# An AdaLN feed-forward kernel on one Trainium2 core: other engines and banks for the last two of 32 tiles

## The chip, the core and the metric

The kernel runs on one core of a Trainium2 chip. Its engines run instruction streams of their own and meet only at semaphores: TensorE (PE, matmuls, with PEld for its weight loads), VectorE (DVE), ScalarE (ACT), GpSimd (POOL) and SyncE (SP), which here does nothing but issue DMAs, in order, on its queue (SPq). SBUF is the on-chip memory of 128 partitions; PSUM holds matmul results in eight banks of 128x512 f32. The metric is the device time of one execution in microseconds (us).

## What is computed

Tokens are a matrix of 4096 rows (2 batches of 2048) by 512. A conditioned matrix product gives h; a feed-forward block with ternary weights and activations rounded to 8-bit steps per row follows, and x is added back.

```python
def _act_quant(x):
    scale = 127.0 / jnp.clip(jnp.max(jnp.abs(x), axis=-1, keepdims=True), 1e-05)
    xq = jnp.clip(jnp.round(x * scale), -128.0, 127.0) / scale
    ...
def _bitlinear(x, w):
    return jnp.einsum('bsi,oi->bso', _act_quant(x), _weight_quant(w))
gate = jax.nn.silu(_bitlinear(x, w_gate))
up = _bitlinear(x, w_up)
return _bitlinear(gate * up, w_down)
...
x = x + _L0_ffn_ref(_L0_cond_ref(x, cond_8, L0_cond_weight, ...), ...)
```

w_gate and w_up are 2048 by 512, w_down is 512 by 2048. The step that matters here is the second `_act_quant`: the row maximum over all 2048 columns of gate * up must be known before any of it can be rounded and multiplied by w_down.

## The kernel before

The 4096 rows are 32 tiles of 128 rows. A first phase (to about 125 us) builds the conditioned weights, makes the weights ternary and produces the rounded, transposed activations qT of nearly all tiles. The second phase goes through the tiles, one step each, and every engine has its own hand-written order with semaphore counts; there is no scheduler. The tile index is s, its parity par picks one of two buffers.

In a step each of the four chunks (512 of the 2048 inner columns) goes this way. TensorE (`chunk`, L498) multiplies qT by the gate and the up weights into PSUM banks GATE + c % 2 and UP + c % 2. ScalarE (`silu_chunk`, L269) applies silu to the gate bank. VectorE (`step`, L400) multiplies it with the up bank into `prod` and takes the chunk's absolute maximum (L402). TensorE starts a chunk only when silu and product of two chunks before it are done.

After four chunks VectorE combines the maxima and computes the row's scale in four small operations (L412, L414, L417, L419), rounds `prod` in place in two halves of 1024 columns by adding a large constant (L424), and computes `out_unit` (L426). ScalarE (`convert`, L276) subtracts the constant and writes bf16 into the single buffer `q2`, half by half; in the next step this stands between silu chunks 0 and 1. SyncE (L211) issues one DMA transpose for each half into `q2T`. TensorE (`down`, L508) then does sixteen matmuls into bank DOWN + par, interleaved with the chunks two tiles later. VectorE (`finish_out`, L390) scales that bank and adds x (`x_res`) into `result`; this runs in the middle of the step three tiles later.

SyncE's order around a step s (`step` of the sync block, L205 to L220) is: both transposes of tile s - 1; wait for the result of tile s - 3; its store (L218); the load of x for tile s - 1 into the same buffer (L220). All of it is one queue: an instruction that waits holds all behind it.

For the last tiles nothing differs in the kernel before, but that TensorE runs out of chunks: behind chunk (31, 3) come the down matmuls of tiles 29, 30 and 31 in a row. Names in profile rows: `wc` is the big buffer in which prod, q2, q2T and silu lie, `ps` is PSUM.

Of the kernel before, what the change touches and what calls it, by code (L numbers as in the profile page):

```python
# [7 lines left out]
ALU = mybir.AluOpType  # L8
# [5 lines left out]
TILES = BATCH * SEQ // P  # L14
# [10 lines left out]
COND_BANKS = 8  # L25
LATE = TILES - 2
AHEAD = 11
HSLOTS = 3
# [6 lines left out]

GATE, UP, DOWN, MIX = 0, 2, 4, 6


def build(nc, xT, x, y_col, wcond, mask, bias, w_gate, w_up, w_down, out):
    with ExitStack() as ctx:  # L40
# [3 lines left out]
        def sem(name):  # L44
            return ctx.enter_context(nc.semaphore(name))
# [88 lines left out]
        p_rounded = sem("p_rounded")  # L134
        q2_ready = sem("q2_ready")
        down_psum = sem("down_psum")
        result_ready = sem("result_ready")
# [8 lines left out]
        def _(sp):  # L146
# [58 lines left out]
            def step(s):  # L205
                if 1 <= s <= TILES:
                    if s >= 3:
                        sp.wait_ge(down_psum, s - 2)
                    for half in range(2):
                        sp.wait_ge(q2_ready, 2 * (s - 1) + half + 1)  # L210
                        sp.dma_start_transpose(q2T[:, (s - 1) % 2, 8 * half:8 * half + 8, :],  # L211
                                               q2[:, 1024 * half:1024 * half + 1024]).then_inc(s_q2T[half], 16)
# [15 lines left out]
        def _(pool):  # L228
# [5 lines left out]
            for m in range(3):  # L234
                pool.wait_ge(mean_step, 3 * (m + 1))
                for a in range(PIECES):
                    nc.gpsimd.tensor_scalar(raws[m][:, a], raws[m][:, a], w_inv[:, m:m + 1], ROUND, ALU.mult, ALU.add  # L237
                                            ).then_inc(scaled, 1)

        @block.scalar  # L240
        def _(act):
# [28 lines left out]

            def convert(t, par):
                for half in range(2):
                    act.wait_ge(p_rounded, 2 * t + half + 1)
                    if not (isinstance(t, int) and t == 0):
# [26 lines left out]
            for t in range(LATE):  # L301
                cond_round(t)
                if t in abs_after:
                    abs_sum_piece(*abs_after[t])
            for s in range(TILES):
                step(s, s % 2)
            convert(TILES - 1, 1)

        @block.vector
        def _(dve):  # L310
# [74 lines left out]
            def finish_out(t, par):  # L385
                dve.wait_ge(down_psum, t + 1)
                dve.wait_ge(s_xres[par], 8 * (t - par) + 16)
                if not (isinstance(t, int) and t < 2):
                    dve.wait_ge(s_store[par], 8 * (t - par))
                nc.vector.scalar_tensor_tensor(out=result[:, par], in0=ps[:, DOWN + par], scalar=column(out_unit, t),  # L390
                                               in1=x_res[:, par], op0=ALU.mult, op1=ALU.add).then_inc(result_ready, 1)

            def step(s, par, late=None, out_on=True):
# [27 lines left out]
                dve.wait_ge(p_col, 5 * s + 4)  # L421
                for half in range(2):
# [35 lines left out]
            step(LATE, 0)  # L458
            step(LATE + 1, 1)
            for t in range(TILES - 3, TILES):  # L460
                finish_out(t, t % 2)

        @block.tensor
        def _(pe):
# [36 lines left out]
            def down(t, par, c):  # L501
                if c == 0 and not (isinstance(t, int) and t < 2):
                    pe.wait_ge(result_ready, t - 1)
                if c % 2 == 0:
                    pe.wait_ge(s_q2T[c // 2], 16 * t + 16)
                for j in range(4):
                    k = 4 * c + j
                    ins = nc.tensor.matmul(ps[:, DOWN + par], q2T[:, par, k], tern_down[:, k], start=(k == 0), stop=(k == KI - 1))  # L508
                if c == 3:
# [107 lines left out]
```

## Time and profile before

| | us |
|---|---|
| median of 3 runs | 477.2 (477.15 to 477.87) |
| profiled execution, device time | 477.17 |
| its span in the trace | 475.4 |
| TensorE busy | 456.8 (96%) |
| VectorE busy | 355.7 (75%) |
| ScalarE busy | 220.0 (46%) |
| GpSimd busy | 26.2 (6%), none of it after 112 |

The span runs from the first instruction to the last; 1.8 us of the device time lie outside it. Busy counts matmuls and vector work, not waits or DMA issues. The chain that ended last is traced back from the last instruction through whatever released each step; it goes through TensorE for 70% of the span, through VectorE for 10%, SyncE's queue 5%, DMA 5%. At the end of the span the chain is: scale of tile 31, rounding, conversion, transpose, sixteen down matmuls, result, store.

### The profile page before, as it was taken

To read this page: it belongs to the slowest core of one execution; us is meant where nothing else is said; L and a number is where in the kernel's file an instruction comes from. 1 tells how busy PE (TensorE), PEld (TensorE's weight loads), DVE (VectorE), ACT (ScalarE), POOL (GpSimd) and SP (SyncE) were. 2 spreads that over 40 slices of the span, in tenths; PEclk is the share of its full clock that TensorE was granted. 3 is DMA by queue.
4 is the path that set the end of the run, shared out by engine and by line. 5 is a ranking of instruction groups with operands and counts; after the bars stand their busy time and mean duration, and the time that the engine had idled before them with its cause. 6 is when DMAs were issued, how large, how long until landed. Compare 5 with 4: busy or idle time off the path is not lost.

```text
span 475.4 us, 6225 instructions
## 1 busy us (share of the span) xinstructions
PE 456.8 (96%) x1830; PEld 201.6 (42%) x1862; DVE 355.7 (75%) x700; ACT 220.0 (46%) x290; POOL 26.2 (6%) x19
## 2 busy tenths in 40 slices
PE   4899989999999999999999999999999999999996
PEld 0234434444444444444444444444444444444432
DVE  0315699898588888777887877788787878788782
ACT  1217964965335554444454444445444344543431
POOL 0000252424000000000000000000000000000000
PEclk9999999999999999999999999999999999999999
DMA  7999999964202244453334444333445433344535
GB/s 258 409 400 415 407 242 265 330 175 94 44 12 55 57 108 114 113 110 88 88 88 109 112 114 107 89 88 88 112 108 114 107 88 88 94 113 106 127 92 133
DMA packets 104304, 69.67 MB, mean 147 GB/s; under 512 B 87264, under 2 KB 87264, under 8 KB 102752
## 3 DMA queue, kind: packets, MB, share of 16 engines
q1 hardware_dynamic: 104288, 69.49, 52.7%
q8 instruction: 6, 0.10, 0.1%
q14 instruction: 10, 0.08, 0.0%
HBM read 40.11 MB, written 8.39 MB: 102 GB/s over the span
## 4 chain that ended last, share of the span: by engine, by line
PE 70%; DVE 10%; SPq 5%; DMA 5%; issue 4%; ACT 4%; POOL 2%; DVEq 0%; ACTq 0%
PE ps L498 40%; PE ps L508 21%; PE ps L467 10%; DMA wc<-w_gate 4%; SPq L157 3%; POOL wc L237 2%; DVE wc L400 2%; DVE h_max L363 1%; DVE h_sb L361 1%; SPq L150 1%; DVE p_part L402 1%; DVE tern_gate L352 1%; ACT wc L269 1%; ACT h_sb L253 1%; DVE wc L424 1%
## 5 line engine op out<-in xcount | busy, mean ns | idle before, releaser
L269 ACT ACTIVATE wc<-ps,gate_unit 128x512 f32<-128x512 f32 x128 | 87.2, 683 | 139.5 <-PE ps L498 139.5
L498 PE MATMUL ps<-tern_up,qT 128*128 128x512 bf16 x510 | 131.2, 379 | 0.1
L498 PE MATMUL ps<-tern_gate,qT 128*128 128x512 bf16 x484 | 127.4, 379 | 4.0 <-DVE wc L400 2.4
L508 PE MATMUL ps<-tern_down,wc 128*128 128x512 bf16 x510 | 129.5, 379 | 1.4 <-DMA wc<-wc 1.3
L400 DVE TENSOR_TENSOR wc<-ps,wc 128x512 f32<-128x512 f32 x128 | 87.9, 687 | 49.1 <-PE ps L498 29.3
L467 PE MATMUL ps<-w_bot,xT_sb 128*128 128x512 f32 x256 | 113.4, 595 | 3.1 <-DVE w_bot L338 1.6
L402 DVE TENSOR_REDUCE p_part<-wc 128x1 f32<-128x512 f32 x128 | 87.8, 686 | 4.4
L276 ACT ACTIVATE wc<-wc 128x1024 bf16<-128x1024 f32 x64 | 64.1, 1049 | 38.3 <-DVE wc L424 38.3
L498 PEld LDWEIGHTS ps<-tern_gate,qT 128*128 (+1 forms) x512 | 49.7, 98 | 67.0 <-issue 9.1
L508 PEld LDWEIGHTS ps<-tern_down,wc 128*128 128x128 bf16 x512 | 50.0, 98 | 62.0 <-DVE result L390 1.7
L498 PEld LDWEIGHTS ps<-tern_up,qT 128*128 (+1 forms) x512 | 50.1, 98 | 60.4
L467 PEld LDWEIGHTS ps<-w_bot,xT_sb 128*128 128x128 f32 x256 | 47.9, 190 | 62.5 <-issue 56.6
L424 DVE TENSOR_SCALAR wc<-wc,p_scale 128x1024 f32<-128x1024 f32 x64 | 45.3, 750 | 1.1
L253 ACT ACTIVATE h_sb<-h_sb,h_inv 128x512 f32<-128x512 f32 x32 | 22.9, 716 | 29.0 <-DVE h_inv L369 29.0
L361 DVE TENSOR_TENSOR h_sb<-ps,bias_sb 128x512 f32<-128x512 f32 x32 | 22.0, 687 | 12.5 <-ACT q_sb L258 7.7
L237 POOL TENSOR_SCALAR wc<-wc,w_inv 128x2048 f32<-128x2048 f32 x12 | 25.4, 2135 | 84.8 <-DVE w_inv L347 84.8
L390 DVE SCALAR_TENSOR_TENSOR result<-ps,out_unit,x_res 128x512 f32<-128x512 f32 x32 | 23.8, 743 | 6.0 <-PE ps L508 6.0
L330 DVE SCALAR_TENSOR_TENSOR w_bot<-ps,half_on,w_bot 128x512 f32<-128x512 f32 x8 | 6.0, 748 | 26.6 <-PE ps L480 26.6
L363 DVE TENSOR_REDUCE h_max<-h_sb 128x1 f32<-128x512 f32 x32 | 22.0, 686 | 1.1
L258 ACT ACTIVATE q_sb<-h_sb 128x512 bf16<-128x512 f32 x32 | 20.2, 630 | 4.8 <-DMA qT<-q_sb 3.8
L480 PE MATMUL ps<-wc,mix_w 128*32 128x512 f32 x64 | 14.3, 701 | 6.7 <-DMA wc<-wcond 6.7
L296 ACT ACTIVATE w_bot<-ps,half_on 128x512 f32<-128x512 f32 x8 | 5.1, 684 | 28.7 <-PE ps L480 28.7
(41 smaller groups left out, 108.5 us busy)
## 6 DMA issues: line engine op xcount, KB each, us to landing
wc<-wcond SPq DMA_DIRECT2D x16, 512.0 KB, 12.2
xT_sb<-xT SPq DMA_DIRECT2D x32, 256.0 KB, 6.5
x_res<-x SPq DMA_DIRECT2D x32, 256.0 KB, 2.8
out<-result SPq DMA_DIRECT2D x32, 256.0 KB, 2.0
wc<-w_gate SPq DMA_DIRECT2D x4, 1024.0 KB, 17.1
wc<-w_up SPq DMA_DIRECT2D x4, 1024.0 KB, 11.7
wc<-w_down SPq DMA_DIRECT2D x4, 1024.0 KB, 6.6
tern_down<-mask SPq DMA_DIRECT2D x8, 256.0 KB, 14.7
```

The source lines that it names most:

```text
L237: nc.gpsimd.tensor_scalar(raws[m][:, a], raws[m][:, a], w_inv[:, m:m + 1], ROUND, ALU.mult, ALU.add).then_inc(scaled, 1)
L253: nc.scalar.activation(h_sb[:, slot], h_sb[:, slot], ACT.Copy, bias=ROUND, scale=h_inv[:, slot:slot + 1]).then_inc(h_rounded, 1)
L269: nc.scalar.activation(silu[:, c % 2], ps[:, GATE + c % 2], ACT.Silu, scale=unit).then_inc(silu_ready, 1)
L276: nc.scalar.activation(q2[:, 1024 * half:1024 * half + 1024], prod[:, par, 1024 * half:1024 * half + 1024], ACT.Copy, bias=-ROUND).then_in ...
L361: nc.vector.tensor_tensor(h_sb[:, slot], ps[:, t % COND_BANKS], bias_sb[:, :], ALU.add).then_inc(h_ready, 1)
L363: nc.vector.tensor_reduce(h_max[:, slot:slot + 1], h_sb[:, slot], AX.X, ALU.max, apply_absolute_value=True).then_inc(h_col, 1)
L400: nc.vector.tensor_tensor(cut, ps[:, UP + c % 2], silu[:, c % 2], ALU.mult).then_inc(prod_ready, 1)
L402: nc.vector.tensor_reduce(p_part[:, par, c:c + 1], cut, AX.X, ALU.max, apply_absolute_value=True).then_inc(part_ready, 1)
L424: nc.vector.tensor_scalar(cut, cut, p_scale[:, par:par + 1], ROUND, ALU.mult, ALU.add).then_inc(p_rounded, 1)
L467: ins = nc.tensor.matmul(ps[:, t % COND_BANKS], xT_sb[:, t % XSLOTS, k], w_bot[:, t // HALF, k], start=(k == 0), stop=(k == KH - 1))
L498: ins = nc.tensor.matmul(ps[:, bank + c % 2], tile, w[:, c, k], start=(k == 0), stop=(k == KH - 1))
L508: ins = nc.tensor.matmul(ps[:, DOWN + par], q2T[:, par, k], tern_down[:, k], start=(k == 0), stop=(k == KI - 1))
```

## The change

It concerns tiles 30 (LATE) and 31 (LAST).

- Tile 30 is rounded by GpSimd, in two halves, instead of VectorE. ScalarE converts its first half behind silu (31, 0), as before, and its second half behind silu (31, 1).
- Tile 31's first half is rounded and converted by VectorE, its second half by ScalarE in two passes. SyncE's transposes wait on new counters for them.
- The down products of tile 30 go to bank GATE (0) and those of tile 31 to bank UP (2), which are free once all silus and products are done; TensorE waits for that instead of an earlier result.
- The result of tile 28, until now in the middle of VectorE's step for tile 31, is computed behind it, with those of tiles 29 to 31.

```diff
+def down_bank(t):
+    if isinstance(t, int) and t >= LATE:
+        return (GATE, UP)[t - LATE]
+    return None
...
 # SyncE, step
-                        sp.wait_ge(q2_ready, 2 * (s - 1) + half + 1)
+                        if s - 1 < LAST:
+                            sp.wait_ge(q2_ready, 2 * (s - 1) + half + 1)
+                        elif half == 0:
+                            sp.wait_ge(q2_last_ready, 1)
+                        else:
+                            sp.wait_ge(q2_ready, 2 * LAST + 1)
...
 # GpSimd, behind its weight rounding
+            pool.wait_ge(p_col, 5 * LATE + 4)
+            for half in range(2):
+                cut = prod[:, 0, 1024 * half:1024 * half + 1024]
+                nc.gpsimd.tensor_scalar(cut, cut, p_scale[:, 0:1], ROUND, ALU.mult, ALU.add).then_inc(p_rounded_pool, 1)
...
 # ScalarE
-            for s in range(TILES):
+            for s in range(LAST):
                 step(s, s % 2)
-            convert(TILES - 1, 1)
+            silu_chunk(LAST, 0)
+            convert(LATE, 0, [0])
+            silu_chunk(LAST, 1)
+            convert(LATE, 0, [1])
+            silu_chunk(LAST, 2)
+            silu_chunk(LAST, 3)
+
+            act.wait_ge(p_col, 5 * LAST + 4)
+            act.wait_ge(part_ready, CH * TILES)
+            nc.scalar.activation(prod[:, 1, 1024:2048], prod[:, 1, 1024:2048], ACT.Copy, bias=ROUND, scale=p_scale[:, 1:2]
+                                 ).then_inc(p_rounded_act, 1)
+            act.wait_ge(p_rounded_act, 1)
+            act.wait_ge(s_q2T[1], 16 * LAST)
+            nc.scalar.activation(q2[:, 1024:2048], prod[:, 1, 1024:2048], ACT.Copy, bias=-ROUND).then_inc(q2_ready, 1)
...
 # VectorE, step
-                for half in range(2):
+                halves = 2
+                if isinstance(s, int):
+                    halves = {LATE: 0, LAST: 1}.get(s, 2)
+                for half in range(halves):
...
+                if isinstance(s, int) and s == LAST:
+                    dve.wait_ge(p_rounded, 2 * LATE + 1)
+                    dve.wait_ge(s_q2T[0], 16 * LAST)
+                    nc.vector.tensor_scalar(q2[:, 0:1024], prod[:, 1, 0:1024], -ROUND, None, ALU.add).then_inc(q2_last_ready, 1)
...
-            step(LATE + 1, 1)
-            for t in range(TILES - 3, TILES):
+            step(LATE + 1, 1, None, False)
+            for t in range(TILES - 4, TILES):
                 finish_out(t, t % 2)
...
 # TensorE, down; finish_out reads the same bank
+                bank = down_bank(t) if down_bank(t) is not None else DOWN + par
+                if c == 0 and isinstance(t, int) and t >= LATE:
+                    pe.wait_ge(silu_ready, CH * TILES)
+                    pe.wait_ge(prod_ready, CH * TILES)
+                elif c == 0 and not (isinstance(t, int) and t < 2):
                     pe.wait_ge(result_ready, t - 1)
```

The changed kernel has other line numbers: L400 becomes L439, L402 L441, L412 to L419 become L451 to L458, L424 L466, L426 L472, L390 L429; on ScalarE L269 becomes L291 and L276 L301; on SyncE L211, L218 and L220 become L227, L234 and L236.

VectorE, from the second chunk of tile 31 to its last, before. L390 is the result of tile 28.

```order
L400 TENSOR_TENSOR wc<-ps,wc 128x512 [waits up_psum,silu_ready]
L402 TENSOR_REDUCE p_part<-wc 128x1 [waits prod_ready]
L390 SCALAR_TENSOR_TENSOR result<-ps,out_unit,x_res 128x512 [waits s_store0,s_xres0,down_psum]
L400 TENSOR_TENSOR wc<-ps,wc 128x512 [waits up_psum,silu_ready]
L402 TENSOR_REDUCE p_part<-wc 128x1 [waits prod_ready]
L400 TENSOR_TENSOR wc<-ps,wc 128x512 [waits up_psum,silu_ready]
```

The result stood between the second and the third chunk. VectorE now, from tile 31's scale to the end of its program (L471 is the conversion of the first half, the first L429 the result of tile 28):

```order
L458 TENSOR_SCALAR p_scale<-p_inv,up_unit 128x1 [waits p_col]
L466 TENSOR_SCALAR wc<-wc,p_scale 128x1024 [waits p_col]
L471 TENSOR_SCALAR wc<-wc 128x1024 [waits s_q2T0,p_rounded]
L472 TENSOR_SCALAR out_unit<-p_unit,w_mean 128x1
L429 SCALAR_TENSOR_TENSOR result<-ps,out_unit,x_res 128x512 [waits s_store0,s_xres0,down_psum]
L429 SCALAR_TENSOR_TENSOR result<-ps,out_unit,x_res 128x512 [waits s_store1,s_xres1,down_psum]
L429 SCALAR_TENSOR_TENSOR result<-ps,out_unit,x_res 128x512 [waits s_store0,s_xres0,down_psum]
L429 SCALAR_TENSOR_TENSOR result<-ps,out_unit,x_res 128x512 [waits s_store1,s_xres1,down_psum]
```

One rounding has become a conversion, and four results instead of three stand behind it. SyncE, the end of its program, now: the transposes of tile 30, then the store of tile 28 and the load of x for tile 30, then the transposes of tile 31.

```order
L227 DMA_TRANSPOSE wc<-wc 128x8x128 [waits q2_ready,down_psum]
L227 DMA_TRANSPOSE wc<-wc 128x8x128 [waits q2_ready]
L234 DMA out<-result 128x512 [waits result_ready]
L236 DMA x_res<-x 128x512
L227 DMA_TRANSPOSE wc<-wc 128x8x128 [waits q2_last_ready,down_psum]
L227 DMA_TRANSPOSE wc<-wc 128x8x128 [waits q2_ready]
L234 DMA out<-result 128x512 [waits result_ready]
L236 DMA x_res<-x 128x512
```

The order of this queue is that of before; only the counter in the fifth row is another. ScalarE, from tile 31's first silu to the end, before:

```order
L269 ACTIVATE wc<-ps,gate_unit 128x512 [waits prod_ready,gate_psum] x4
L276 ACTIVATE wc<-wc 128x1024 [waits s_q2T0,p_rounded]
L276 ACTIVATE wc<-wc 128x1024 [waits s_q2T1,p_rounded]
L269 ACTIVATE wc<-ps,gate_unit 128x512 [waits prod_ready,gate_psum] x3
L276 ACTIVATE wc<-wc 128x1024 [waits s_q2T0,p_rounded]
L276 ACTIVATE wc<-wc 128x1024 [waits s_q2T1,p_rounded]
```

and now:

```order
L291 ACTIVATE wc<-ps,gate_unit 128x512 [waits prod_ready,gate_psum] x4
L301 ACTIVATE wc<-wc 128x1024 [waits s_q2T0,p_rounded_pool]
L291 ACTIVATE wc<-ps,gate_unit 128x512 [waits prod_ready,gate_psum]
L301 ACTIVATE wc<-wc 128x1024 [waits s_q2T1,p_rounded_pool]
L291 ACTIVATE wc<-ps,gate_unit 128x512 [waits prod_ready,gate_psum] x2
L341 ACTIVATE wc<-wc,p_scale 128x1024 [waits part_ready,p_col]
L345 ACTIVATE wc<-wc 128x1024 [waits s_q2T1,p_rounded_act]
```

Silu (31, 1) has moved between the two conversions of tile 30. The first row of each holds the last three silus of tile 30 and the first of tile 31.

## Rows read from the trace of the kernel before

**Rows 1.** The page: span, TensorE's share, granted clock in 40 slices (tenths).
```profile
span 475.4 us, 6225 instructions
...
PE 456.8 (96%) x1830; PEld 201.6 (42%) x1862; DVE 355.7 (75%) x700; ACT 220.0 (46%) x290; POOL 26.2 (6%) x19
...
PEclk9999999999999999999999999999999999999999
```

**Rows 2.** Timeline, seam of tiles 30 and 31: start us, us, engine, line, operation, [idle, releaser].
```profile
453.12 0.69 ACT L269 ACTIVATE wc<-ps,gate_unit 128x512 f32<-128x512 f32 x1 [1.90 <-PE ps L498]
...
453.91 0.21 DVE L419 TENSOR_SCALAR p_scale<-p_inv,up_unit 128x1 f32<-128x1 f32 x1
454.15 1.42 DVE L424 TENSOR_SCALAR wc<-wc,p_scale 128x1024 f32<-128x1024 f32 x2
...
454.94 2.00 ACT L276 ACTIVATE wc<-wc 128x1024 bf16<-128x1024 f32 x2 [1.13 <-DVE wc L424]
...
455.61 0.68 DVE L400 TENSOR_TENSOR wc<-ps,wc 128x512 f32<-128x512 f32 x1
...
456.44 1.02 PE L498 MATMUL ps<-tern_gate,qT 128*128 128x512 bf16 x4 [0.76 <-DVE wc L400]
456.85 1.33 ACT L269 ACTIVATE wc<-ps,gate_unit 128x512 f32<-128x512 f32 x2
...
457.55 0.69 DVE L400 TENSOR_TENSOR wc<-ps,wc 128x512 f32<-128x512 f32 x1 [0.54 <-ACT wc L269]
```

**Rows 3.** Timeline, same columns, rest of tile 31's products.
```profile
458.88 0.74 DVE L390 SCALAR_TENSOR_TENSOR result<-ps,out_unit,x_res 128x512 f32<-128x512 f32 x1
...
459.54 0.68 DVE L400 TENSOR_TENSOR wc<-ps,wc 128x512 f32<-128x512 f32 x1
459.65 0.34 SPq L218 DMA_DIRECT2D out<-result  x1
...
460.04 0.43 SPq L220 DMA_DIRECT2D x_res<-x  x1
460.12 7.07 PE L508 MATMUL ps<-tern_down,wc 128*128 128x512 bf16 x32
...
462.94 0.21 DVE L419 TENSOR_SCALAR p_scale<-p_inv,up_unit 128x1 f32<-128x1 f32 x1
```

**Rows 4.** Timeline, same columns, the tail.
```profile
463.19 1.42 DVE L424 TENSOR_SCALAR wc<-wc,p_scale 128x1024 f32<-128x1024 f32 x2
...
464.64 0.74 DVE L390 SCALAR_TENSOR_TENSOR result<-ps,out_unit,x_res 128x512 f32<-128x512 f32 x1
465.10 2.61 SPq L211 DMA_TRANSPOSE wc<-wc  x2
...
468.46 3.61 PE L508 MATMUL ps<-tern_down,wc 128*128 128x512 bf16 x16 [1.28 <-DMA wc<-wc]
...
472.12 0.75 DVE L390 SCALAR_TENSOR_TENSOR result<-ps,out_unit,x_res 128x512 f32<-128x512 f32 x1 [4.14 <-PE ps L508]
```

**Rows 5.** Lines L237 and L338, whole span: count, duration ns min/median/max, first and last start.
```profile
L237 POOL TENSOR_SCALAR wc<-wc,w_inv x12: 1975/1977/2922, 56.1 to 109.8; 128x2048 f32<-128x2048 f32 x12
...
L338 DVE TENSOR_TENSOR w_bot<-w_bot,tern_down x8: 679/692/2370, 14.0 to 63.4; 128x512 f32<-128x512 f32 x8
```

**Rows 6.** A load's issue; landing: L211; last two L220; page's x_res; L165 at 108.76, 110.0.
```profile
108.39 0.33 SPq L150 DMA_DIRECT2D xT_sb<-xT  x1
...
DMA to landing us min/median/max: 3.1/3.2/4.4
...
DMA to landing us min/median/max: 3.0/3.5/4.1
...
x_res<-x SPq DMA_DIRECT2D x32, 256.0 KB, 2.8
...
DMA to landing us min/median/max: 2.9/2.9/2.9
...
DMA to landing us min/median/max: 2.5/2.5/2.5
```

More of the change, by code:

```diff
@@ L26 @@
 LATE = TILES - 2
+LAST = TILES - 1
 AHEAD = 11
@@ L135, in build @@
         q2_ready = sem("q2_ready")
+        p_rounded_pool = sem("p_rounded_pool")
+        p_rounded_act = sem("p_rounded_act")
+        q2_last_ready = sem("q2_last_ready")
         down_psum = sem("down_psum")
@@ L269, in silu_chunk, with convert @@
                 nc.scalar.activation(silu[:, c % 2], ps[:, GATE + c % 2], ACT.Silu, scale=unit).then_inc(silu_ready, 1)
-            def convert(t, par):
-                for half in range(2):
-                    act.wait_ge(p_rounded, 2 * t + half + 1)
+            def convert(t, par, halves=range(2)):
+                for half in halves:
+                    if t == LATE:
+                        act.wait_ge(p_rounded_pool, half + 1)
+                    else:
+                        act.wait_ge(p_rounded, 2 * t + half + 1)
                     if not (isinstance(t, int) and t == 0):
@@ L389, in finish_out @@
                     dve.wait_ge(s_store[par], 8 * (t - par))
-                nc.vector.scalar_tensor_tensor(out=result[:, par], in0=ps[:, DOWN + par], scalar=column(out_unit, t),
+                bank = down_bank(t) if down_bank(t) is not None else DOWN + par
+                nc.vector.scalar_tensor_tensor(out=result[:, par], in0=ps[:, bank], scalar=column(out_unit, t),
                                                in1=x_res[:, par], op0=ALU.mult, op1=ALU.add).then_inc(result_ready, 1)
@@ L421, in step @@
                 dve.wait_ge(p_col, 5 * s + 4)
-                for half in range(2):
+                halves = 2
+                if isinstance(s, int):
+                    halves = {LATE: 0, LAST: 1}.get(s, 2)
+                for half in range(halves):
                     cut = prod[:, par, 1024 * half:1024 * half + 1024]
@@ L501, in down @@
             def down(t, par, c):
-                if c == 0 and not (isinstance(t, int) and t < 2):
+                bank = down_bank(t) if down_bank(t) is not None else DOWN + par
+                if c == 0 and isinstance(t, int) and t >= LATE:
+                    pe.wait_ge(silu_ready, CH * TILES)
+                    pe.wait_ge(prod_ready, CH * TILES)
+                elif c == 0 and not (isinstance(t, int) and t < 2):
                     pe.wait_ge(result_ready, t - 1)
@@ L507, in down @@
                     k = 4 * c + j
-                    ins = nc.tensor.matmul(ps[:, DOWN + par], q2T[:, par, k], tern_down[:, k], start=(k == 0), stop=(k == KI - 1))
+                    ins = nc.tensor.matmul(ps[:, bank], q2T[:, par, k], tern_down[:, k], start=(k == 0), stop=(k == KI - 1))
                 if c == 3:
```

## The prediction

> **What bounds the kernel now.** First the page: TensorE is busy 96% of the span [rows 1], so the body is a matmul stream and only its seams can give anything. The change touches the last two of 32 tiles, so all that follows is read from the timeline of the last 23 us. Times below are microseconds of the span, with tile and 512-column chunk as (31, 2).
>
> In the seam between tile 30 and tile 31 [rows 2] VectorE rounds tile 30 in two halves (454.15, 1.42 for both), and only then multiplies (31, 0) at 455.61; TensorE waits 0.76 for that product. ScalarE converts both halves of tile 30 (454.94, 2.00), and this, not TensorE, holds back silu (31, 1) to 456.85 and product (31, 1) to 457.55. Next [rows 3] the result of tile 28 takes VectorE 0.74 at 458.88, in front of product (31, 2) at 459.54. The scale of tile 31 is ready at 463.15 (462.94 and 0.21). Then comes the tail [rows 4]: rounding 463.19, conversion on ScalarE, SyncE's transposes issued from 465.10, 3.2 to land [rows 6], tile 31's sixteen down matmuls at 468.46 after a wait of 1.28, 3.61 long, the result at 472.12, its store. TensorE finished the down matmuls of tiles 29 and 30 at 467.19 (460.12 and 7.07) [rows 3]. So the end of the span hangs on one thing: when the first transpose of tile 31 lands. A microsecond won earlier counts only if that transpose is issued earlier.
>
> **The change, part by part.** I rebuild the schedule from 454.12, the end of tile 30's scale, up to which nothing changes.
>
> GpSimd rounds tile 30. No row shows a 128x1024 rounding there; the nearest is its 128x2048 one, 1977 ns in the median and 2922 ns at most [rows 5]. By proportion a half costs 0.99 to 1.46; I take 1.05, near the median with a little for the start, since nothing in the seam resembles the stretch of the 2922. With some 0.07 for the handover the halves are done at 455.25 and 456.25, where VectorE's were at 454.90 and 455.57. VectorE is free 1.3 earlier, product (31, 0) goes to about 454.3, and TensorE's wait of 0.76 goes.
>
> ScalarE takes tile 30's conversions apart. The first runs 455.30 to 456.30 (half of 2.00 [rows 2]), silu (31, 1) starts at 456.28 instead of 456.85, product (31, 1) at 456.98 instead of 457.55: 0.57 won. The second conversion runs 456.9 to 457.9 and silu (31, 2) 457.9 to 458.55, so product (31, 2) starts at 458.6, against 459.54: 0.94 won. Most of the further gain is the result of tile 28 that no longer stands in front of it. From there VectorE is bound by itself as before (459.54 to 463.15 is 3.61): the scale of tile 31 is ready at 462.2, a win of 0.95.
>
> Tile 31 is shared. VectorE rounds the first half (0.75, half of the pair of 1.42 and its overlap [rows 4]) and converts it itself. That form has no row; the rounding of as many elements on the same engine is the nearest, 0.71 to 0.75. So the first half is ready at 462.2 + 0.03 + 0.75 + 0.03 + 0.72 = 463.7, where it was 465.05 before: 1.35 won on the data. ScalarE's half, two passes of 1.0 to 1.15 by the conversion's row, is ready at about 464.4; it is wanted only by the second transpose, which SyncE can't issue before 465 anyway, so it costs nothing. If both passes took 0.6 longer it still would.
>
> The last results go behind the chain, and SyncE's queue does not move with them. In its order the store of tile 28 and the load of x for tile 30 stand ahead of tile 31's transposes. Before, the result of tile 28 was there at 459.62 and both were issued at 459.65 and 460.04 [rows 3], five microseconds before they could be in the way. Now VectorE computes that result after its conversion: the small op for out_unit and then 463.75 to 464.5 (0.74 [rows 3]). SyncE waits for it, issues the store at 464.53, the load at 464.92 and gets to the first transpose 0.48 later (0.43 and the gap), at 465.40. That is 0.30 later than 465.10. The 1.35 won is eaten by 0.8 for the result and 0.87 for the two issues.
>
> What is queued is also in flight. Before, the DMA engines had nothing else when the transposes went out. Now 512 KB of store and load start less than 0.9 ahead. The nearest row: the transpose at 108.76, issued 0.37 behind a 256 KB load, landed after 2.9, one with only another transpose in front after 2.5 [rows 6]: 0.4 to 0.5. With two transfers ahead, from nothing (if they are through by the time the transposes' data start) to 1.3, the most by which a load's landing was late in this neighbourhood (4.1 against 2.8 [rows 6]). I take 0.5, since the second transfer here stands about as far ahead as the load there. The Trainium skill, page "DMA: Bandwidth & Descriptors", section "Issuing engines are not separate DMA queues", says that transfers run on the same 16 engines and interleave; by that alone the delay would be the share of the 512 KB not yet moved, and the measured 0.4 agrees that it is not zero.
>
> The down products of tiles 30 and 31 in the gate and up banks. The banks are free when product (31, 3) is done, about 460.6; tile 30's down matmuls start near 463.0. So the new wait costs nothing, and tile 31's no longer depend on a result. They had not been waiting for one. Tile 30's down matmuls end near 466.6 by the 0.6 that TensorE is earlier. Queued behind the moved results are only later results: tile 30's x is issued at 464.92 and at 2.8 to 4.1 lands by 469.0, tile 31's is issued about 468.7 + 0.5 and lands, at 3.0 as the quicker of the last two did [rows 6], by 472.2; the matmuls end later than that.
>
> **Sum.** Against the profiled execution's 477.17 (span 475.4, 1.8 around it; the median of the runs is 477.2): first transpose issued 0.30 later, landing 0.5 late, the rest of the tail unchanged. 477.17 + 0.80 = 477.97, so **478.0**, 0.17% above.
>
> **The rivals.**
> - **Port sharing at GpSimd.** The row for L338 shows a product with two SBUF operands at 679 ns, and up to 2370 ns beside GpSimd's rounding, whose own longest was 2922 ns [rows 5]. If the product (31, 0) met tile 30's rounding in this way, each half would take 1.46: both waits on GpSimd grow, the first conversion by 0.4, the second by 0.8, of which the chain takes 0.8: 478.8. Against it: L400 reads PSUM and only one SBUF operand. I give it 0.1. The skill's "GPSIMD Engine Reference", overview table, names VectorE instructions with two SBUF inputs, or in a two-port mode, as what contends; by that rule L400 and L402 would not, and the row of L338 agrees with it.
> - **Collision at the upper end (slower).** The store of tile 28 and the load for tile 30 delay the first transpose by more than 0.65, the point from which the total passes 0.2%. At 1.3 it is 477.17 + 0.3 + 1.3 = 478.8. For it: two transfers and not one, and the late load. Against: all 64 of these transposes land in 3.2 in the median and 4.4 at most [rows 6], and the nearest row for a load in front gives 0.4. 0.26.
> - **The queue doesn't block (faster).** If SyncE reached the transposes as soon as the first half was ready, they would be issued at 463.75 and the end would be 1.35 earlier: 475.8 (TensorE's down matmuls of tile 30, done at 466.6, would just be out of the way). For it only that my reading of the order could be wrong; the order lists the store, with its wait on the result counter, in front. 0.05.
> - **The change doesn't reach the end.** Collision of nothing to 0.2: 477.4 to 477.7, within 0.2%. 0.2.
> - **The clock.** TensorE would idle 2.6 between tile 30 and 31's down matmuls instead of 1.28. The granted clock stands at 9 tenths or more of the upper level (2.4 GHz) in all slices, the one with that 1.28 too [rows 1]. Were it to fall to 1.2 GHz, the sixteen matmuls take double, 3.5 more: 481.4. 0.02. The skill's page "TensorE: Matmul & The Clock Gate", section "Why this matters for your kernels", warns of idle gaps between bursts; no row of this case shows a fall.
>
> **How the numbers follow.** Forecast (issue +0.3, collision 0.2 to 0.65): 0.37, all within 0.2% (0.95 us, about what can be told from no change here). With the case that doesn't reach the end, same is 0.57. Slower: 0.26 + 0.1 + 0.02 = 0.38. Faster 0.05. The range goes from 477.1 (no collision, GpSimd at its fastest, and the runs' own spread) to 478.9 (either slower case); the clock and the free queue stay out.
>
> **What would show it.** Right: in the profile after, the product (31, 0) starts near 454.3 and TensorE's wait of 0.76 is gone; the scale of tile 31 ends near 462.2; SyncE waits for the result of tile 28 until about 464.5, and the first transpose is issued near 465.4 and takes 3.4 to 4.0 to land; TensorE waits over 2 us before the last sixteen matmuls. Wrong: GpSimd's halves far from 1.05, the transposes issued before 464.8 or after 466, a landing of 3.2 flat, or a lower clock over the last matmuls. What would most of all make the forecast wrong is a collision outside 0.2 to 0.65.

## The result, and the profile after

| | before | after |
|---|---|---|
| median, 17 executions each | 477.67 (476.89 to 478.4) | 479.44 (477.73 to 482.13) |
| profiled execution | 477.17 | 477.85 |
| its span | 475.4 | 475.9 |

The ratio is 1.0040, with a 95% interval of 1.0031 to 1.0049: the change makes the kernel 0.4% slower, 1.8 us. The forecast was 478.0, with 477.1 to 478.9. It was 0.8 above a time of 477.17 for the kernel before; here before has 477.67 in the median, so 0.5 of the miss of 1.5 (479.44 against the sum's 477.97) is the starting point, and the rest is that the change costs 1.8 and not 0.8. Two things stand out. The profiled execution is close to the forecast, and it is one of the quickest of its kind. And the executions of after spread over 4.4 us, those of before over 1.5.

The page of after: span, TensorE, granted clock. The mean granted clock over this execution is 1.000.

```profile
span 475.9 us, 6226 instructions
...
PE 456.5 (96%) x1830; PEld 201.5 (42%) x1862; DVE 354.4 (74%) x698; ACT 220.0 (46%) x290; POOL 28.4 (6%) x21
...
PEclk9999999999999999999999999999999999999999
```

Timeline of after, seam and tail (start us, us, engine, line, operation, [idle before and what ended it]). They answer to [rows 2] to [rows 4]. The whole body of this execution is 0.16 later (scale of tile 30 at 454.07, there 453.91); subtract that to compare.

```profile
454.07 0.21 DVE L458 TENSOR_SCALAR p_scale<-p_inv,up_unit 128x1 f32<-128x1 f32 x1
...
454.38 2.21 POOL L260 TENSOR_SCALAR wc<-wc,p_scale 128x1024 f32<-128x1024 f32 x2 [342.48 <-DVE p_scale L458]
454.45 0.68 DVE L439 TENSOR_TENSOR wc<-ps,wc 128x512 f32<-128x512 f32 x1
...
457.19 0.69 DVE L439 TENSOR_TENSOR wc<-ps,wc 128x512 f32<-128x512 f32 x1 [1.34 <-ACT wc L291]
...
458.72 0.69 DVE L439 TENSOR_TENSOR wc<-ps,wc 128x512 f32<-128x512 f32 x1
...
462.12 0.21 DVE L458 TENSOR_SCALAR p_scale<-p_inv,up_unit 128x1 f32<-128x1 f32 x1
...
463.16 0.69 DVE L471 TENSOR_SCALAR wc<-wc 128x1024 bf16<-128x1024 f32 x1
...
463.89 1.40 DVE L429 SCALAR_TENSOR_TENSOR result<-ps,out_unit,x_res 128x512 f32<-128x512 f32 x2
464.66 0.34 SPq L234 DMA_DIRECT2D out<-result  x1
465.05 0.43 SPq L236 DMA_DIRECT2D x_res<-x  x1
465.58 2.63 SPq L227 DMA_TRANSPOSE wc<-wc  x2
...
469.02 3.61 PE L558 MATMUL ps<-tern_down,wc 128*128 128x512 bf16 x16 [2.20 <-DMA wc<-wc]
...
472.67 0.75 DVE L429 SCALAR_TENSOR_TENSOR result<-ps,out_unit,x_res 128x512 f32<-128x512 f32 x1 [4.02 <-PE ps L558]
```

Read down to 462.12 it is a gain: product (31, 0) starts at 454.45 for 455.61 in [rows 2], product (31, 2) at 458.72 for 459.54, the scale of tile 31 ends at 462.33 for 463.15. At 463.85 (463.16 and 0.69) the first half is ready for its transpose (before 465.05). Then the result of tile 28 (first of the pair at 463.89), its store (464.66) and the load (465.05) go first, and the transposes are issued at 465.58, where it was 465.10. TensorE waits 2.20 for them, not 1.28. The last sixteen matmuls take 3.61 as before, and the last result starts at 472.67 for 472.12, which is 0.39 later once the 0.16 is taken off. All this was forecast, and by more (0.8 for the end), so it does not explain 1.8.

What the profile of this one execution can't show is in the granted clock of the others. Of these 17 executions 5 have a mean granted clock of 0.999 or 1.000 and a median of 478.57, and 12 have 0.993 to 0.996 and a median of 479.77. Over both series of after (these 17, and 12 of the same kernel below) 10 have 0.999 or 1.000, a median of 477.92 and 479.11 at most. The other 19 have 0.993 to 0.996, a median of 479.70 and 479.22 at least. In 79 executions of before that ran beside the experiments, the lowest was 0.999.

### The profile page after: what moved, and what is told of

The parts are those of the page before. It is cut to its first block, busy times and chain, and to the rows that moved or that the text cites. A ratio compares the mean times of both kernels' runs of the same rounds, so it can differ in the third digit from the quotient of the medians.

```text
span 475.9 us, 6226 instructions
## 1 busy us (share of the span) xinstructions
PE 456.5 (96%) x1830; PEld 201.5 (42%) x1862; DVE 354.4 (74%) x698; ACT 220.0 (46%) x290; POOL 28.4 (6%) x21
## 4 chain that ended last, share of the span: by engine, by line
issue 74%; DVE 6%; SPq 5%; DMA 5%; PE 4%; POOL 4%; ACT 2%; POOLq 0%; DVEq 0%; ACTq 0%
DMA wc<-w_gate 4%; POOL wc L253 4%; PE ps L513 3%; SPq L168 3%; DVE h_max L401 1%; DVE h_sb L399 1%; SPq L161 1%; DVE tern_gate L390 1%; PE ps L558 1%; DMA wc<-wc 1%; SPq L164 1%; DVE tern_up L390 0%; SPq L172 0%; ACT tern_gate L269 0%; ACT tern_up L269 0%
## 5 line engine op out<-in xcount | busy, mean ns | idle before, releaser
L291 ACT ACTIVATE wc<-ps,gate_unit 128x512 f32<-128x512 f32 x128 | 87.2, 682 | 138.7 <-PE ps L544 138.7
L439 DVE TENSOR_TENSOR wc<-ps,wc 128x512 f32<-128x512 f32 x128 | 87.9, 687 | 50.1 <-PE ps L544 29.3
L441 DVE TENSOR_REDUCE p_part<-wc 128x1 f32<-128x512 f32 x128 | 87.8, 686 | 4.4
L301 ACT ACTIVATE wc<-wc 128x1024 bf16<-128x1024 f32 x62 | 62.2, 1049 | 34.9 <-DVE wc L466 33.3
L466 DVE TENSOR_SCALAR wc<-wc,p_scale 128x1024 f32<-128x1024 f32 x61 | 43.2, 750 | 1.1
L429 DVE SCALAR_TENSOR_TENSOR result<-ps,out_unit,x_res 128x512 f32<-128x512 f32 x32 | 23.7, 742 | 6.6 <-PE ps L558 4.0
L260 POOL TENSOR_SCALAR wc<-wc,p_scale 128x1024 f32<-128x1024 f32 x2 | 2.2, 1120 | 342.5 <-DVE p_scale L458 342.5
```

The lines of the kernel that those rows point to most:

```text
L291: nc.scalar.activation(silu[:, c % 2], ps[:, GATE + c % 2], ACT.Silu, scale=unit).then_inc(silu_ready, 1)
L301: nc.scalar.activation(q2[:, 1024 * half:1024 * half + 1024], prod[:, par, 1024 * half:1024 * half + 1024], ACT.Copy, bias=-ROUND).then_in ...
L439: nc.vector.tensor_tensor(cut, ps[:, UP + c % 2], silu[:, c % 2], ALU.mult).then_inc(prod_ready, 1)
L441: nc.vector.tensor_reduce(p_part[:, par, c:c + 1], cut, AX.X, ALU.max, apply_absolute_value=True).then_inc(part_ready, 1)
```

## The experiments

Theory C: TensorE's longer idle time before tile 31's down matmuls brings its clock down in most executions. Theory V: something else varies, GpSimd or the meeting of store, load and transposes, and the extra time stands in front of those matmuls. All ratios are to the kernel before on the same chip. "Fallen" below is a mean granted clock of 0.996 or less over the span. A mean of 0.999 can hold a fall too, but one that costs nothing: the profiled execution of d2_pool30 (0.999) has its last matmul end at 471.60, and its clock goes down behind it.

```profile
471.60:473.50 1.90, 0.01 (x1) 0.00 (x0) 0.75 (x1) 0.00 (x0) 0.00 (x0) 1.00 0.12 46
...
474.00:474.90 0.90, 0.00 (x0) 0.00 (x0) 0.00 (x0) 0.00 (x0) 0.00 (x0) 0.50 0.00 0
```

The columns are: stretch, its us; busy us and count of PE, PEld, DVE, ACT, POOL; granted clock; DMA share; GB/s. The fall stands at about 473.8, some 2.2 us behind the last matmul. In the profile of b2_gap it stands some 2.5 behind (475.5, the last matmul ends at 472.99). In those of before and after the clock is at 1.00 to the end of the span, 3.3 behind the last matmul. So the same idle time ends in a fall in one execution and not in another.

### a0_after: the changed kernel again

> The changed kernel as it is, to see where the time beyond the forecast goes. The profiled execution of it took 477.85 us with a granted clock of 1.0, the median of all 479.44, with a mean granted clock of 0.993 to 0.996 in most executions. Theory C (clock): TensorE now stands idle 2.2 us before tile 31's down matmuls and the granted clock falls to its lower level around them; then this run is 479.4 in the median, mean clock near 0.996, and where the profiled execution is such a one, its last sixteen down matmuls take about 2 us longer than 3.61 while all up to there is as in the other profile. Theory V (variation elsewhere: the roundings on GpSimd, or how store, load and transposes meet in the DMA engines, vary from execution to execution): 479.4 too, but with the extra time in front of the last matmuls, as a later landing or a later scale.

479.29 in the median of 12 (477.62 to 480.38), ratio 1.0032 (1.0019 to 1.0046). Seven fallen, at 479.22 to 480.38; five not, at 477.62 to 478.51. The profiled one was of the five, with an idle time of 2.42 and 3.61 for the matmuls, so where the time goes was not seen here; that the two groups don't overlap was.

### a1_fill: nine idle matmuls in the gap

```diff
             for t in range(LATE - 1, TILES):
+                if t == LAST:
+                    for k in range(9):
+                        nc.tensor.matmul(ps[:, MIX], q2T[:, 0, k], tern_down[:, k], start=True, stop=True)
```

> The changed kernel with nine more 128x512 matmuls on TensorE between tile 30's and tile 31's down matmuls, into a bank that nobody reads; they take 1.95 of the 2.2 us that TensorE waits. Theory C: TensorE is no longer idle, the clock stays at its upper level in every execution, median 477.9, 1.5 us below the changed kernel. Theory V: nothing else is altered, so 479.4 stays.

477.74 (477.23 to 478.89), ratio 1.0009 (1.0000 to 1.0019), no execution of 12 fallen. Timeline of a1_fill: the nine matmuls, then tile 31's, which wait 0.48 (one of the sixteen is missing from the trace).

```profile
465.42 2.65 SPq L227 DMA_TRANSPOSE wc<-wc  x2
...
466.50 2.10 PE L630 MATMUL ps<-tern_down,wc 128*128 128x512 bf16 x9
...
469.09 3.61 PE L558 MATMUL ps<-tern_down,wc 128*128 128x512 bf16 x15 [0.48 <-DMA wc<-wc]
```

Matmuls whose result nobody reads make the kernel 1.5 us faster, at a start of the last matmuls (469.09) that is no earlier than in after (469.02). Nothing of GpSimd, the queue or the transfers was altered, so theory V is out as the cause of the 1.5. What is left to before, 0.5, fits the transpose, which is issued and lands later in the profile; no run takes that part by itself.

### a2_order: the transposes first in SyncE's queue

```diff
-                if s >= 3:
-                    par = (s - 3) % 2
...
+                if s >= 3 and s != LAST:
+                    for r in ((s - 1, s) if s == LAST + 1 else (s,)):
+                        par = (r - 3) % 2
```

> The changed kernel with one thing altered on SyncE: the transposes of tile 31 are issued ahead of the store of tile 28 and the load of x for tile 30. If SyncE's order is what gave back the gain, the first transpose is issued near 464.0 instead of 465.6, TensorE waits under 0.6 us before the last matmuls, and the end comes 1.2 to 1.6 earlier than in the profiled execution of the changed kernel: 476.4, if tile 31's x lands in time. Theory C: clock 1.0 in every execution, so the median is 476.4 too, 3 us below the changed kernel. Theory V: median near 478.

476.79 (476.35 to 477.35), ratio 0.9988 (0.9980 to 0.9997). Timeline of a2_order, the tail: the first half ready, store and load now behind the transposes, the last matmuls, the last result.

```profile
462.92 0.69 DVE L472 TENSOR_SCALAR wc<-wc 128x1024 bf16<-128x1024 f32 x1
...
466.35 0.58 SPq L235 DMA_DIRECT2D out<-result  x1
466.97 0.44 SPq L237 DMA_DIRECT2D x_res<-x  x1
...
467.02 3.61 PE L559 MATMUL ps<-tern_down,wc 128*128 128x512 bf16 x16 [0.43 <-DMA wc<-wc]
...
471.34 0.75 DVE L430 SCALAR_TENSOR_TENSOR result<-ps,out_unit,x_res 128x512 f32<-128x512 f32 x1 [0.60 <-DMA x_res<-x]
```

With the two transfers out of the way the last matmuls start at 467.02, after an idle time of 0.43. So SyncE's order did give the gain back. The result at 471.34 waits 0.60 for x of tile 31, whose load is now later; that is the next bound. None of 12 was at 0.996. Three show 0.997 or 0.998 and took 476.35 to 477.34, inside the range of the others; where in them the clock was lower was not seen.

### b1_late28: the moved result alone, on the kernel before

```diff
-            step(LATE + 1, 1)
-            for t in range(TILES - 3, TILES):
+            step(LATE + 1, 1, None, False)
+            for t in range(TILES - 4, TILES):
```

> The kernel before with one part of the change alone: the result of tile 28 behind VectorE's step for tile 31. The scale of tile 31 is 0.64 earlier, but SyncE's transposes wait behind the result, store and load: first transpose issued about 0.54 later than before, TensorE idle about 1.9 instead of 1.28. Without a fall of the clock 477.8. Theory C: the clock falls in a part of the executions, so the median lies between 477.8 and 479.5, with a wide spread. Theory V: 477.8 and a narrow spread, since GpSimd and the two-pass half are as before.

478.66 (478.04 to 480.07), ratio 1.0032 (1.0020 to 1.0043). The issue is late as expected, but the idle time isn't 1.9 in one piece. Timeline of b1_late28: the scales of tiles 30 and 31, and the tail:

```profile
453.77 0.21 DVE L419 TENSOR_SCALAR p_scale<-p_inv,up_unit 128x1 f32<-128x1 f32 x1
...
462.34 0.21 DVE L419 TENSOR_SCALAR p_scale<-p_inv,up_unit 128x1 f32<-128x1 f32 x1
...
464.05 1.40 DVE L390 SCALAR_TENSOR_TENSOR result<-ps,out_unit,x_res 128x512 f32<-128x512 f32 x2
...
464.85 3.63 PE L508 MATMUL ps<-tern_down,wc 128*128 128x512 bf16 x16 [1.25 <-DVE result L390]
...
465.73 2.61 SPq L211 DMA_TRANSPOSE wc<-wc  x2
...
469.38 3.61 PE L508 MATMUL ps<-tern_down,wc 128*128 128x512 bf16 x16 [0.91 <-DVE result L390]
```

Tile 30's down matmuls wait 1.25 for the result of tile 28, since with the old banks they write where it is read; the last sixteen then wait 0.91, by their start for the transpose, which landed 3.5 after its issue (the profile names the result of tile 30, which they don't need). That is what the new banks are for. In this kernel the wait of 1.25 is hidden, since the transpose lands later still; with the transpose out of the way as in a2_order, where the last matmuls start at 467.02, it would count, because tile 30's end only at 468.48 here. That is an estimate, no run has it. Between the two scales lie 8.57, for 9.03 before. None was at 0.996, one at 0.997 (480.07, the slowest). Yet the median lies 0.6 above the profiled 478.08, and one execution took 480.01 at a clock of 1.000. This spread without a fall was not expected by theory C. Here theory V has a part: something that is not the clock can cost up to 2 us, and what it is stays open. The transposes' landing behind store and load varies, as below, but by less than that.

### c1_gap: the gap 1.2 longer

```diff
                 dve.wait_ge(p_col, 5 * s + 4)
+                if isinstance(s, int) and s == LAST:
+                    for i in range(2):
+                        nc.vector.tensor_tensor(h_sb[:, i], h_sb[:, 2], h_sb[:, 2], ALU.mult)
```

> The changed kernel with two more 128x512 products on VectorE ahead of tile 31's rounding, which nobody reads; they move rounding, result of tile 28 and transposes 1.3 us back, so TensorE idles 3.5 to 3.7 us before its last sixteen matmuls instead of 2.2 to 2.4. Theory C (the clock falls after that idle time): it falls in every execution, mean granted clock 0.993 to 0.996 in all, and the profile shows it: the last sixteen matmuls at the lower level (1.2 GHz) take up to 3.5 us longer than 3.61. Time 1.3 above the undisturbed changed kernel (477.8 in its two profiled executions) plus 2 to 3.5: 481 to 482.5, with no execution near 479.1. Without a clock effect: 479.1 in all.

480.73 in the median of 6 (478.79 to 481.42), ratio 1.0067 (1.0051 to 1.0082). Four fallen, at 480.57 to 481.42; two not, at 478.79 and 479.05. The two groups lie 2 apart, much as in after, but I had expected a fall in every execution. Timeline of c1_gap, the last matmuls of an execution that did not fall:

```profile
469.95 3.61 PE L561 MATMUL ps<-tern_down,wc 128*128 128x512 bf16 x16 [3.37 <-DMA wc<-wc]
```

The idle time is 3.37, for 2.20 in after, and it can still pass without a fall.

### c2_fill4: four filler matmuls

The diff is that of a1_fill, with 4 for 9.

> The changed kernel with four extra matmuls instead of the nine of the earlier filler, so that TensorE idles about 1.5 us, near the 1.28 of the kernel before, in which no execution out of 35 showed a mean clock under 0.999. Theory C: no fall either, median 477.8 as with nine. If any idle time of over about a microsecond is enough, a part of the executions is at 0.996 and 479.4.

478.16 (477.77 to 478.81), ratio 1.0015 (1.0006 to 1.0024), none of 11 fallen. Timeline of c2_fill4:

```profile
466.54 1.03 PE L630 MATMUL ps<-tern_down,wc 128*128 128x512 bf16 x4
...
469.15 3.61 PE L558 MATMUL ps<-tern_down,wc 128*128 128x512 bf16 x16 [1.58 <-DMA wc<-wc]
```

Four matmuls are enough, with 1.58 of idle time left. The chip is the one on which c1_gap has its falls.

### c3_mid28: the result of tile 28 back in the middle

```diff
-            step(LATE + 1, 1, None, False)
-            for t in range(TILES - 4, TILES):
+            step(LATE + 1, 1)
+            for t in range(TILES - 3, TILES):
```

> The changed kernel with one part undone: the result of tile 28 back in the middle of VectorE's step for tile 31. Then its store and the load of x for tile 30 are out of SyncE's way early, at the price of 0.6 us on VectorE's chain. First transpose issued near 464.5 (the kernel before 465.1, changed 465.5), TensorE idle 1.2 to 1.4, clock 1.0 throughout, median 476.7, that is 0.5 under the kernel before. If the moved result was not the harmful part: 479.3 as changed.

476.76 (475.83 to 477.73), ratio 0.9984 (0.9975 to 0.9993), none of 11 fallen. Timeline of c3_mid28. The body of this execution is 0.56 earlier than that of before, so intervals are to be compared.

```profile
453.35 0.21 DVE L458 TENSOR_SCALAR p_scale<-p_inv,up_unit 128x1 f32<-128x1 f32 x1
...
457.80 0.74 DVE L429 SCALAR_TENSOR_TENSOR result<-ps,out_unit,x_res 128x512 f32<-128x512 f32 x1
...
461.86 0.21 DVE L458 TENSOR_SCALAR p_scale<-p_inv,up_unit 128x1 f32<-128x1 f32 x1
...
463.66 2.61 SPq L227 DMA_TRANSPOSE wc<-wc  x2
...
467.00 3.61 PE L558 MATMUL ps<-tern_down,wc 128*128 128x512 bf16 x16 [0.90 <-DMA wc<-wc]
...
470.66 0.75 DVE L429 SCALAR_TENSOR_TENSOR result<-ps,out_unit,x_res 128x512 f32<-128x512 f32 x1 [3.76 <-PE ps L558]
```

From the scale of tile 30 to that of tile 31 it is 8.51 here, 8.05 in after, 9.03 before. So the result in the middle costs 0.46 of the chain, and GpSimd's rounding brings 0.52. From the scale of tile 30 to the first transpose it is 10.31, in after 11.51, before 11.19. One part undone, and the kernel is no longer slower than before but faster.

### c4_early_x: the transposes first, and x for the last two tiles early

```diff
+                if s in (4, 5):
+                    sp.dma_start(h_sb[:, s - 4], x[LATE + s - 4]).then_inc(s_xlast[s - 4], 16)
-                if s >= 3:
...
+                if s >= 3 and s != LAST:
+                    for r in ((s - 1, s) if s == LAST + 1 else (s,)):
...
-                        if s - 1 < TILES:
+                        if r - 1 < LATE:
...
+                tail = isinstance(t, int) and t >= LATE
+                if tail:
+                    dve.wait_ge(s_xlast[t - LATE], 16)
```

> The changed kernel with the transposes of tile 31 first in SyncE's queue (as in the earlier run of that order: 476.79 in the median, its last result waiting 0.6 us for x of tile 31) and with x for tiles 30 and 31 loaded at steps 4 and 5 into a buffer that is free by then. The last result then waits for TensorE alone, at about 470.7 instead of 471.34: 475.9, with less spread than the 476.35 to 477.35 of that run. If the spread there came from elsewhere than the late loads, it stays a microsecond wide.

476.31 (475.65 to 477.13), ratio 0.9979 (0.9970 to 0.9987), none of 11 fallen. Timeline of c4_early_x:

```profile
463.78 2.60 SPq L228 DMA_TRANSPOSE wc<-wc  x2
...
467.11 3.61 PE L566 MATMUL ps<-tern_down,wc 128*128 128x512 bf16 x16 [0.44 <-DMA wc<-wc]
...
470.76 0.75 DVE L437 SCALAR_TENSOR_TENSOR result<-ps,out_unit,h_sb 128x512 f32<-128x512 f32 x1 [1.05 <-PE ps L566]
```

The last result no longer waits for x. This has the lowest ratio of all, 0.2% under before, though its interval overlaps those of a2_order and c3_mid28. The spread is 1.5 wide (1.0 in a2_order), so it was not the late loads; before has 1.8 beside it.

### d1_gap_long: a gap long enough for a profile with the fall in it

```diff
                 dve.wait_ge(p_col, 5 * s + 4)
+                if isinstance(s, int) and s == LAST:
+                    nc.vector.tensor_reduce(p_part[:, 0, 0:1], terns[0].rearrange("p c n -> p (c n)"), AX.X, ALU.max)
```

> The changed kernel with one long maximum on VectorE (128x8192, about 8.6 us by 0.96 columns a nanosecond as in its other reductions) ahead of tile 31's rounding, so TensorE idles some 11 us before the last sixteen matmuls. It is there to have a profile with the lower clock in it. Theory C: the clock has fallen in every execution, the profiled one too; the granted clock over the end of the span is about 0.5 and the sixteen matmuls take up to 3.5 us longer than 3.61, less if the clock rises again among them. Time 477.8 + 8.6 + 2 to 3.5 = 488.4 to 489.9. Without a clock effect 486.4.

489.16 (487.94 to 489.44), ratio 1.0236 (1.0220 to 1.0251), all three fallen (0.988 and 0.989). Timeline of d1_gap_long, and under it its stretches (columns as above):

```profile
474.06 2.61 SPq L227 DMA_TRANSPOSE wc<-wc  x2
...
477.53 5.19 PE L560 MATMUL ps<-tern_down,wc 128*128 128x512 bf16 x16 [10.83 <-DMA wc<-wc]
```

```profile
466.70:470.00 3.30, 0.01 (x1) 0.00 (x0) 3.30 (x1) 0.00 (x0) 0.00 (x0) 1.00 0.00 0
...
470.00:471.00 1.00, 0.00 (x0) 0.00 (x0) 1.00 (x2) 0.00 (x0) 0.00 (x0) 0.76 0.00 0
...
476.00:478.00 2.00, 0.47 (x2) 0.22 (x3) 0.75 (x1) 0.00 (x0) 0.00 (x0) 0.50 1.19 247
478.00:480.00 2.00, 2.00 (x6) 0.65 (x5) 0.00 (x0) 0.00 (x0) 0.00 (x0) 0.50 0.97 284
480.00:481.00 1.00, 1.00 (x4) 0.39 (x3) 0.00 (x0) 0.00 (x0) 0.00 (x0) 0.62 0.45 172
481.00:482.00 1.00, 1.00 (x7) 0.47 (x5) 0.00 (x0) 0.00 (x0) 0.00 (x0) 1.00 0.01 2
```

The last matmul of tile 30 ends at 466.71. The clock stays at 1.00 to 470, falls within the next microsecond, and stands at 0.50 (1.2 GHz) when the last sixteen begin. They take 5.19 instead of 3.61: not double, because it rises again at 480 to 481, some 3 us into them. So a fall costs these matmuls 1.6 here, and the two groups of after lie 1.8 apart. This fall came 3.8 us behind the last matmul, later than the 2.2 that after has; that it can come sooner is seen at the ends of the spans of d2_pool30 and b2_gap (2.2 and 2.5). An estimate for after from the means: 0.996 over 477.5 us is some 3.8 us at the lower level, so the fall would stand within the gap, about a microsecond or less ahead of the sixteen matmuls, if the clock comes back some 3 us into them as here.

### b2_gap: the kernel before with nothing but a longer gap

```diff
                 dve.wait_ge(p_col, 5 * s + 4)
+                if isinstance(s, int) and s == LATE + 1:
+                    for i in range(2):
+                        nc.vector.tensor_tensor(h_sb[:, i], h_sb[:, 2], h_sb[:, 2], ALU.mult)
```

> The kernel before, with nothing of the change, and two products on VectorE that nobody reads ahead of tile 31's rounding: the tail moves back 1.3 us and TensorE idles 2.6 us in place of 1.28. Theory C, that the idle time alone brings the clock down and no other part of the change is needed: about two executions in three show a mean granted clock of 0.995 or 0.996 and take 2 us more, so 478.5 for those without and 480.4 for those with a fall, median near 480. If GpSimd's rounding, the two-pass half or the new banks have a part in it: no falls, 478.5.

479.28 in the median of 5 (478.09 to 480.35), ratio 1.0039 (1.0026 to 1.0053). Two of five fallen, at 479.55 and 480.35, and none of the 15 executions of before on that chip; three not, at 478.09 to 479.28. Timeline of b2_gap:

```profile
466.04 2.61 SPq L211 DMA_TRANSPOSE wc<-wc  x2
...
469.38 3.61 PE L511 MATMUL ps<-tern_down,wc 128*128 128x512 bf16 x16 [2.46 <-DMA wc<-wc]
```

The idle time is 2.46, and that alone, without GpSimd's rounding, new banks or shared tile, brings the falls. Five executions are few to tell 2 in 5 from 2 in 3.

### d2_pool30: GpSimd's rounding alone

c3_mid28 without the new banks and the shared tile 31:

```diff
+            pool.wait_ge(p_col, 5 * LATE + 4)
+            for half in range(2):
+                cut = prod[:, 0, 1024 * half:1024 * half + 1024]
+                nc.gpsimd.tensor_scalar(cut, cut, p_scale[:, 0:1], ROUND, ALU.mult, ALU.add).then_inc(p_rounded_pool, 1)
...
+            silu_chunk(LAST, 0)
+            convert(LATE, 0, [0])
+            silu_chunk(LAST, 1)
+            convert(LATE, 0, [1])
```

> The kernel before with one part of the change alone: GpSimd rounds tile 30 and ScalarE converts its halves apart. Tile 31 is rounded by VectorE and converted by ScalarE as before, the result of tile 28 stays in the middle, the banks are the old ones. From the scale of tile 30 to that of tile 31 it took 9.03 us before, 8.05 in the changed kernel, and 8.51 where the result of tile 28 was put back in the middle; here 8.51 too. The first transpose is then issued 0.5 earlier than before, TensorE idles about 1.2, the clock stays up: 476.7, equal to the run with the result put back minus at most 0.4 for the shared tile 31. If the rounding on GpSimd were what harms: over 477.5.

476.76 (476.17 to 478.87), ratio 0.9989 (0.9978 to 1.0000). Timeline of d2_pool30:

```profile
453.97 0.21 DVE L449 TENSOR_SCALAR p_scale<-p_inv,up_unit 128x1 f32<-128x1 f32 x1
...
462.48 0.21 DVE L449 TENSOR_SCALAR p_scale<-p_inv,up_unit 128x1 f32<-128x1 f32 x1
...
464.65 2.61 SPq L220 DMA_TRANSPOSE wc<-wc  x2
...
467.99 3.61 PE L542 MATMUL ps<-tern_down,wc 128*128 128x512 bf16 x16 [1.27 <-DMA wc<-wc]
```

Again 8.51 between the two scales, and the first transpose 10.68 after the first of them: 0.51 less than before. The shared tile 31 brings another 0.37 in the profile (10.31 in c3_mid28), but nothing that the medians show. One execution of 11 was fallen (0.996, 478.87). The profiled one, not fallen, has an idle time of 1.27. So about 1.3 is not quite safe, as far as one case can say.

## Why the prediction was wrong

Taken together, by the idle time of TensorE ahead of the last sixteen matmuls in the profile:

| kernel | idle us | fallen |
|---|---|---|
| a2_order, c4_early_x, a1_fill | 0.43 to 0.48 | 0 of 35 |
| c3_mid28 | 0.90 | 0 of 11 |
| d2_pool30 | 1.27 | 1 of 11 |
| before | 1.28 | 0 of 79 |
| b1_late28 | 0.91, and 1.25 ahead of tile 30's | 0 of 12 |
| c2_fill4 | 1.58 | 0 of 11 |
| after, a0_after | 2.20, 2.42 | 19 of 29 |
| b2_gap | 2.46 | 2 of 5 |
| c1_gap | 3.37 | 4 of 6 |
| d1_gap_long | 10.83 | 3 of 3 |

Each idle time is that of one profiled execution, and but for d1_gap_long that one was not fallen.

Point by point, with 0.16 taken off the times of after:

- **What bounds the kernel: right.** The end hangs on the first transpose of tile 31; every kernel above that issued it earlier than before had a ratio under 1 (d2_pool30 with an interval that reaches 1.0000).
- **GpSimd's rounding: right.** 2.21 for both halves, 1.12 each, where 1.05 was taken and 0.99 to 1.46 allowed. L439 beside it took 0.68, so VectorE was not held; the rival of port sharing did not happen. (By the prediction's own terms the second half ends at 456.30, not 456.25; nothing hangs on it.)
- **The chain to the scale of tile 31: right, in sum and in its split.** 462.17 for the forecast 462.2. The forecast took 0.57 from GpSimd's rounding and the conversions taken apart, and the further 0.38 for the most part from the moved result. The runs have 0.52 for the first (c3_mid28, d2_pool30) and 0.46 for the second (c3_mid28 against after, b1_late28 against before). That it is 0.46 and not the whole 0.74 is in the forecast too.
- **The queue: right.** First half ready at 463.69 (forecast 463.7), first transpose issued at 465.42 (465.40). a2_order and c3_mid28 show that this order is what gave the gain back.
- **The collision: right in kind, too large.** The transpose landed after 3.3 in the profile of after (below), against 3.2 before: 0.1, not 0.5, and outside the 0.2 to 0.65 that the prediction had named as what would most of all make it wrong. In the profiles of the other kernels with store and load just ahead it is 3.3 (c1_gap, d1_gap_long), 3.5 (a0_after, a1_fill, b1_late28) and 3.6 (c2_fill4), where they are out of the way 3.2. So 0.1 to 0.4, and it varies; the transpose behind an xT load was a fair row for the upper end.
- **The sum: near for the executions without a fall, and partly by luck.** In the profile of after the issue is 0.32 later and the last matmuls 0.40, where the forecast had 0.8. The profiled execution took 0.68 longer than that of before, but 0.16 of it is its later body. The median without a fall, 477.92 over both series, is near the 477.97 of the forecast; in the first series alone it is 478.57.

Landing of the first transpose of tile 31 in after, and in b1_late28:

```profile
DMA to landing us min/median/max: 3.3/3.3/3.3
...
DMA to landing us min/median/max: 3.5/3.5/3.5
```

- **The banks: right** that they cost nothing. What was not said is that with the moved result and the old banks tile 30's matmuls would wait for it (1.25 in b1_late28).
- **The clock: the step that failed.** The sum puts it at nothing, with "the rest of the tail unchanged"; it was listed as a rival with a chance of 0.02 and 3.5 us. It happened in 12 executions of 17, in 19 of 29 over both series, and the groups lie 1.8 apart (479.70 and 477.92; 1.2 in the first series alone). The chance was put so low because the clock had stayed up over an idle time of 1.28 and through 40 slices of one profile. But 2.6 forecast (2.2 measured) was a longer idle time than any that the tail had shown, and a stretch that had never been seen can't be cleared by one that is half as long. The price was too high: in d1_gap_long the clock comes back before the sixteen are through, and they take 1.6 longer. With two in three fallen, the median of all lies in the upper group. The Trainium skill's warning about idle gaps between bursts of matmuls ("TensorE: Matmul & The Clock Gate", section "Why this matters for your kernels") had been cited and put aside; the runs agree with it, and already at gaps shorter than it names, though not in every execution: a gap alone was enough (b2_gap), and filling it was enough (a1_fill).

What stays open: the spread of b1_late28 at a full clock (a1_fill has 478.62 and 478.89 at 1.000 too), and what decides in which execution the clock falls. No execution of after with a fall has a profile here, so a fall that reaches the matmuls is seen only in d1_gap_long; for after it is inferred from the mean granted clock, from a1_fill and from b2_gap.

## What to carry to other kernels

Before moving a result "behind the chain", read what its store and its next load stand in front of: on an in-order DMA queue the late result holds up every transfer behind it, and the chain with it. Where a change lengthens TensorE's idle time ahead of its last matmuls, treat the clock as a likely case and not a remote one, look at the granted clock of every execution and not at one profile, and try a few filler matmuls. A part that harms can hide one that helps (c3_mid28 is 0.2% faster than before, after 0.4% slower): take the change apart before throwing it away.

## What was not expected of the hardware

With an idle time on TensorE of 2.2 to 2.4 us in the profiles, two executions of three had a lower mean clock (0.993 to 0.996 over the span); with 3.37, two of six had none. Behind the last matmul the clock fell after 2.2 us (d2_pool30), 2.5 (b2_gap) and, in the long gap, 3.8 (d1_gap_long), and was still up after 3.3 in before and after. Back at work at 1.2 GHz, TensorE was at 2.4 GHz again some 3 us later (d1_gap_long). A transpose issued 0.53 behind a 256 KB load and 0.92 behind a 256 KB store landed only 0.1 later, and 0.1 to 0.4 later in the other kernels of that order. GpSimd rounded 128x1024 f32 in 1.12 us beside VectorE's product out of PSUM, which took 0.68 as before.
